# The rounding number of the FFN weights' FP4 quantisation, taken from a bit mask and a maximum on VectorE to a quadratic on ScalarE

## The chip, the cores and the metric

One core of one Trainium2 chip. The metric is the device time of one execution in microseconds (us), the median of several. The engines are called PE (TensorE, matmul), PEld (its weight loads), DVE (VectorE), ACT (ScalarE), POOL (GpSimd) and SP (SyncE, which issues the transfers here).

## The reference

One block of a network on x of shape (4, 1024, 256), with a context of shape (4, 154, 192):

```
x = x + attention(layernorm(x), ctx)      # 16 heads of 64, 154 keys
x = x + ffn(layernorm(x))                 # 256 -> 704 -> 256
ffn(x) = fp4_linear(silu(fp4_linear(x, w_gate)) * fp4_linear(x, w_up), w_down)

def fp4_quant_dequant(x):                 # on activations and on weights, blocks of 16
    scale = max(max|xb| / 6, 1e-12)
    xn = xb / scale
    q = GRID[searchsorted(MID, |xn|)] * sign(xn) * scale
    # GRID 0, .5, 1, 1.5, 2, 3, 4, 6
```

So every weight matrix of the FFN (704x256 twice, 256x704 once) is quantised once per launch: divided by its block's scale, rounded to a grid whose step is 0.5 below 2, 1 from 2 to 4 and 2 from 4 to 6, and multiplied by the scale again.

## The kernel before, in words

The 4096 rows are 32 tiles of 128, called t here. Each engine has its own instruction stream, written out in one order by hand, and semaphores tie the streams together. A tile's attention takes 8 slots, k = 0 to 7, one for each pair of heads; slot 0.4 is slot 4 of tile 0. In a slot PE makes the scores of a pair (line 1286), DVE takes their negated maximum (`largest_score`, L909), ACT makes the exponentials (L670), DVE inverts their sums (L892), POOL multiplies (`normalise`, L521). PE turns the probabilities around (L1298), ACT copies them from PSUM (`weights_hi`, tile `pT_hi`, L597), DVE writes what that copy lost (`weights_lo`, tile `pT_lo`, L783), and PE attends with both (L1313 to L1315). The same pair of high part on ACT and low part on DVE, L597 and L783, takes every product that PE must read again: `q_hi` and `q_lo`, `B_sb`, `WGU`, `WD`. The layer norm, the FFN's gate and up products and its down product of earlier tiles are put between the slots; each engine runs one stream, so what stands behind a waiting instruction waits too.

The quantisation of the FFN's weights lies beside the attention of tiles 0 and 1 and the first slot of tile 2, in 8 chunks, c0 to c7: six of 128x512 (gate and up side by side) and two of 128x704 (down). Slots are counted on from tile 0. `RAW_AT = [0, 1, 3, 5, 6, 8, 11, 14]` says in which slot a chunk's block scales are made on DVE (`chunk_scales`: L810, L816, L818). One slot later, so in slots 0.1, 0.2, 0.4, 0.6, 0.7, 1.1, 1.4 and 1.7, DVE divides (`chunk_divide`, L824) and makes the rounding number c(n) of each element n (`chunk_rounder`: `power`, L830, keeps the exponent bits; `rounder`, L835, multiplies by 1.5*2^22 and takes the maximum with 1.5*2^22). POOL then adds c, subtracts c and multiplies by the scale (`round_chunk`, helper `fp4`: L486, L490, L492); in tile 0 in the same slot, in tile 1 in the slot after. Adding and subtracting c rounds n to the step of c's binade. The chunk alternates between two tiles for c, `hc` and `hn`. Later PE turns the chunk around (L1163), and ACT and DVE split it into `WGU` or `WD` (`chunk_hi`, `chunk_lo`), in the slots of `TURN_AT = [3, 4, 5, 7, 9, 12, 14, 15, 18, 19]`.

The orders that matter to the change, for a slot in which a chunk is divided:

- ACT, tile 0: exponentials (L670), `weights_hi` of pair k-2 (L597), layer norm 1 out (L626, slots 2 and 4), `xT_hi` (slot 6), `q_hi`, the halves of V, K and B for this batch, `chunk_hi`.
- ACT, tile 1: `weights_hi` of pair k-3, `q_hi`, [layer norm 2 out in slot 5], exponentials, layer norm 1 out (slot 4), `chunk_hi`.
- DVE, tile 0: L909, L824, L892, L830, L835, `pT_lo`, layer norm statistics, `q_lo`, `chunk_scales` of the next chunk, the low parts of B, `chunk_lo`.
- DVE, tile 1: L892, `pT_lo`, L909, `q_lo`, `chunk_lo`, statistics, L824, L830, L835, `chunk_scales`.
- POOL, tile 1: L521 of pair k-1, then the chunk divided one slot earlier.

The FFN's activations go through the same `power` and `rounder` on DVE in every tile; that isn't touched.

Of the kernel before, what the change touches and what calls it, by code (L numbers as in the profile page):

```python
# [6 lines left out]
ACT = mybir.ActivationFunctionType  # L7
# [6 lines left out]
BLOCK = 16  # L14
# [9 lines left out]
def xattn_ffn_kernel(nc: bass.Bass, x, ctx_768, Wq, Wk, Wv, Wo, bo, w_gate, w_up, w_down, out):  # L24
# [31 lines left out]
    with ExitStack() as stack:  # L56
# [3 lines left out]
        def sem(name):  # L60
            return stack.enter_context(nc.semaphore(name))
# [30 lines left out]
        small = sb("small", [P, 24])  # L92
        ln = [[small[:, 10 * i + a:10 * i + b] for a, b in ((0, 6), (6, 8), (8, 9), (9, 10))] for i in range(2)]
        st1, mv1, rs1, nm1 = ln[0]
        st2, mv2, rs2, nm2 = ln[1]
        pow_arg, minus = small[:, 20:21], small[:, 21:22]

        x1_both = sb("x1_both", [P, 2, C])
        x1 = [x1_both[:, i, :] for i in range(2)]
# [55 lines left out]
        st_y = [sem("st_y0"), sem("st_y1")]  # L155
        pad_p, ident_p, pow_p, kpad_p = (sem(n) for n in ("pad_p", "ident_p", "pow_p", "kpad_p"))
        pre_mm, pre_ev, wq_hi, wq_lo, ppad_v = (sem(n) for n in ("pre_mm", "pre_ev", "wq_hi", "wq_lo", "ppad_v"))
        raw_v, raw_p, raw_mm, raw_hi, raw_lo = (sem(n) for n in ("raw_v", "raw_p", "raw_mm", "raw_hi", "raw_lo"))
        k_mm, k_hi, k_lo, v_mm, v_ev = (sem(n) for n in ("k_mm", "k_hi", "k_lo", "v_mm", "v_ev"))
        b_mm, b_hi, b_lo = sem("b_mm"), sem("b_hi"), sem("b_lo")  # L160
        ln1_v, ln1_p, xln1_a = sem("ln1_v"), sem("ln1_p"), sem("xln1_a")
# [309 lines left out]
        def _(pool):  # L471
# [1 line left out]
            pool.wait_ge(ident_p, 1)  # L473
            pool.affine_select(out=ident[:, :], in_=ident[:, :], compare_op=ALU.not_equal, fill=1.0,
                               base=0, pattern=[[-1, P]], channel_multiplier=1).then_inc(ident_p, 1)
            for v, value in ((pow_arg, -0.5), (minus, -1.0)):
                pool.memset(v, value).then_inc(pow_p, 1)
            pool.memset(hn[:, F:FP], 0.0).then_inc(pad_p, 1)

# [22 lines left out]
                pool.wait_ge(done, before + 3)  # L502
                pool.tensor_tensor(nm, nm, rs, ALU.mult).then_inc(done, 1)

            pool.wait_ge(pow_p, 2)
            for n in range(2):
                rstd(mv1, rs1, nm1, (ln1_v, 3 * n + 3), ln1_p, 4 * n)
                pool.memset(K_sb[n][:, :, :].bitcast(F32), 0.0).then_inc(kpad_p, 1)
# [85 lines left out]
        def _(act):  # L594
# [85 lines left out]
            def first(t, setup):  # L680
                for k in range(SLOTS):
                    exponentials(t, k)
                    if k >= 2:
                        weights_hi(t, k - 2)
                    if k == 2:
                        layer_norm1_out(2, 0)
                    if k == 4:
                        layer_norm1_out(t + 3, 1 - t)
                    if k == 6:
                        hi_part(xT_all(0), parts(xT_bank(setup), 4), (xT_mm, 2), xT_hi)  # L690
                    if q_unit(t, t, k) is not None:
                        q_hi_part(t, q_unit(t, t, k))
                    for job in jobs_at(setup, k):
                        take_hi(job, 0)
                    if t == 0 and k == 0:
                        act.wait_ge(pre_mm, CTX_T)
                        for r in range(2, CTX_T):
                            context(r)
                    if turn_at(t, k, 0) is not None:
                        chunk_hi(turn_at(t, k, 0))  # L700

            def step(pair, par, own=True, before=True, gate=True, down=True, out_=True, ahead=True, queries=True,
# [3 lines left out]
                for k in range(SLOTS):  # L706
# [72 lines left out]
        def _(dve):  # L779
# [142 lines left out]
            def first(t, setup):  # L922
                for k in range(SLOTS):
# [23 lines left out]
            def step(pair, par, own=True, before=True, gate=True, down=True, out_=True, ahead=True, queries=True,  # L947
# [3 lines left out]
                for k in range(SLOTS):  # L951
# [551 lines left out]
```

## Time and profile before

| | |
|---|---|
| runs | 870.67, 871.01, 872.89 us, median 871.01 |
| profiled execution | 872.43 us, of which the span from first to last instruction is 870.6 us |
| busy share of the span | PE 96%, DVE 82%, POOL 62%, ACT 60% |
| granted PE clock | 0.988 of full speed on average |
| PE busy in 40 equal slices | 7877899999999999999999999999999999999986 |
| DVE busy in 40 equal slices | 4889788878787888877878888887777888888886 |

The digits are tenths of a slice of 21.8 us. In the first four slices PE isn't full, from the sixth it is. The chain of work that ended last is followed back from the last instruction, at each step to what released it; "idle ... until" and "[0.40 <-ACT ...]" name what ended an engine's idle time. Neighbouring instructions of one engine overlap in the records by about 0.1 us.

### The profile page before, as it was taken

The numbers are of one execution on the slowest core, as the hardware profiler recorded it, in microseconds if no ns is written. First come the engines' busy times: TensorE is split into PE (matmuls) and PEld (weight loads), VectorE is DVE, ScalarE is ACT, GpSimd is POOL, SyncE is SP. The second block draws the span as 40 slices with busy tenths as digits, with TensorE's granted clock in tenths as the row PEclk, the third lists the DMA queues.
The fourth block names the chain that finished last, engine by engine and source line by source line (L and its number), as shares of the span: only waits on it lengthen the run. The fifth ranks groups of instructions, "written<-read, shape, count | busy, mean of one in ns | idle before, by whom it ended". The sixth has DMA issues, their size and how long they took to land.

```text
span 870.6 us, 19198 instructions
## 1 busy us (share of the span) xinstructions
PE 832.2 (96%) x6302; PEld 807.1 (93%) x6302; DVE 710.1 (82%) x2155; ACT 524.8 (60%) x1868; POOL 541.3 (62%) x810
## 2 busy tenths in 40 slices
PE   7877899999999999999999999999999999999986
PEld 7766899999999999999998999999998999999985
DVE  4889788878787888877878888887777888888886
ACT  5554566666676666666666666667656666665530
POOL 3768577765455766665653766665554666666644
PEclk8999999999999999999999999999999999999998
DMA  6320000002010000001111000000200000000000
GB/s 180 103 64 7 8 19 14 26 14 55 15 43 26 13 26 8 25 14 26 43 43 26 14 25 13 26 14 7 62 7 26 7 26 14 19 14 14 7 7 19
DMA packets 20756, 24.30 MB, mean 28 GB/s; under 512 B 2061, under 2 KB 18869, under 8 KB 20661
## 3 DMA queue, kind: packets, MB, share of 16 engines
q1 hardware_dynamic: 19573, 22.04, 8.9%
q8 instruction: 52, 0.85, 0.4%
q10 hardware_dynamic: 1088, 1.05, 0.4%
q14 instruction: 43, 0.35, 0.1%
HBM read 18.89 MB, written 4.19 MB: 27 GB/s over the span
## 4 chain that ended last, share of the span: by engine, by line
PE 81%; DVE 13%; issue 2%; ACT 2%; POOL 1%; DMA 1%; SPq 0%; DVEq 0%; ACTq 0%
PE ps_g L1333 12%; PE ps_s L1286 11%; PE ps_q L1241 10%; PE ps_t L1298 8%; PE ps_o L1313 7%; PE ps_o L1315 7%; PE ps_o L1314 7%; PE ps_g L1197 3%; PE ps_m L1163 3%; PE ps_m L1347 3%; PE ps_m L1349 3%; PE ps_m L1348 2%; PE ps_g L1186 2%; PE ps_q L1186 1%; DVE pT_lo L783 1%
## 5 line engine op out<-in xcount | busy, mean ns | idle before, releaser
L521 POOL TENSOR_TENSOR probs<-probs,rsum 128x308 f32<-128x308 f32 x256 | 180.6, 706 | 214.9 <-DVE rsum L892 214.4
L670 ACT ACTIVATE probs<-ps_s,negmax 128x154 f32<-128x154 f32 x512 | 195.0, 387 | 196.9 <-DVE negmax L909 195.7
L909 DVE TENSOR_REDUCE negmax<-ps_s 128x2 f32<-128x308 f32 x256 | 121.0, 473 | 76.3 <-PE ps_s L1286 75.2
L1313 PE MATMUL ps_o<-B_sb,pT_lo 128*128 128x256 f32 x640 | 180.8, 282 | 0.8 <-DVE x_both L1013 0.5
L1315 PE MATMUL ps_o<-B_sb,pT_hi 128*128 128x256 f32 x640 | 180.5, 282 | 0.0
L1314 PE MATMUL ps_o<-B_sb,pT_hi 128*128 128x256 f32 x640 | 180.3, 282 | 0.0
L783 DVE TENSOR_TENSOR pT_lo<-ps_t,pT_hi 128x256 fp32r<-128x256 f32 (+1 forms) x256 | 122.9, 480 | 30.4 <-ACT pT_hi L597 30.3
L1333 PE MATMUL ps_g<-WGU,xqT_hi 128*128 128x352 f32 x504 | 131.9, 343 | 0.3 <-DVE eh L1036 0.3
L1298 PE MATMUL ps_t<-ident,probs 128*128 128x128 f32 x640 | 113.0, 274 | 16.7 <-DVE pT_lo L783 14.5
L1313 PEld LDWEIGHTS ps_o<-B_sb,pT_lo 128*128 128x128 f32 x640 | 120.8, 189 | 1.3 <-issue 0.7
L1315 PEld LDWEIGHTS ps_o<-B_sb,pT_hi 128*128 128x128 f32 x640 | 121.3, 190 | 0.0
L1314 PEld LDWEIGHTS ps_o<-B_sb,pT_hi 128*128 128x128 f32 x640 | 121.2, 189 | 0.0
L597 ACT ACTIVATE pT_hi<-ps_t 128x256 fp32r<-128x256 f32 (+1 forms) x256 | 111.4, 435 | 6.6 <-PE ps_t L1298 3.4
L670 ACT ACTIVATION_READ_ACCUMULATOR probs<-ps_s,negmax 128x1 f32 x512 | 100.9, 197 | 0.0
L1298 PEld LDWEIGHTS ps_t<-ident,probs 128*128 128x128 f32 x640 | 74.6, 140 | 22.8 <-issue 17.6
L1286 PE MATMUL ps_s<-K_hi,q_lo 128*128 128x308 f32 x256 | 87.1, 340 | 0.0
L1333 PEld LDWEIGHTS ps_g<-WGU,xqT_hi 128*128 128x128 f32 x504 | 82.0, 189 | 0.6 <-DVE eh L1036 0.5
L1241 PE MATMUL ps_q<-xT_hi,Wq_lo 128*128 128x256 f32 x254 | 79.1, 312 | 3.5 <-DVE q_lo L783 2.0
L486 POOL TENSOR_TENSOR hn<-hn,hc 128x704 f32<-128x704 f32 x31 | 52.9, 1707 | 45.6 <-DVE hc L835 45.6
L1333 PE MATMUL ps_g<-WGU,xqT_lo 128*128 128x352 f32 x252 | 81.2, 322 | 0.0
L1286 PE MATMUL ps_s<-K_hi,q_hi 128*128 128x308 f32 x256 | 77.9, 304 | 0.0
L1286 PE MATMUL ps_s<-K_lo,q_hi 128*128 128x308 f32 x256 | 77.8, 304 | 0.0
(236 smaller groups left out, 2199.3 us busy)
## 6 DMA issues: line engine op xcount, KB each, us to landing
xa<-in_x_dram SPq DMA_DIRECT2D x33, 128.0 KB, 2.1
xr<-in_x_dram SPq DMA_DIRECT2D x32, 128.0 KB, 2.0
out_dram<-y_xn SPq DMA_DIRECT2D x30, 128.0 KB, 1.7
W_sb<-in_L_xattn_Wk_dram SPq DMA_DIRECT2D x3, 768.0 KB, 5.7
W_sb<-in_L_xattn_Wv_dram SPq DMA_DIRECT2D x2, 768.0 KB, 6.2
probs<-in_L_xattn_Wq_dram ACTq DMA_DIRECT2D x4, 256.0 KB, 4.9
Wo_sb<-in_L_xattn_Wo_dram SPq DMA_DIRECT2D x1, 1024.0 KB, 6.4
W_sb<-in_L_xattn_Wv_dram SPq DMA_DIRECT2D x2, 384.0 KB, 3.5
```

The lines of the kernel that those rows point to most:

```text
L521: pool.tensor_tensor(unit, unit, rsum[:, 2 * u:2 * u + 2].unsqueeze(2) .to_broadcast([P, 2, M]), ALU.mult).then_inc(norm_p, 1)
L597: act.activation(dst, src, ACT.Copy).then_inc(done, 1)
L670: ins = act.activation(probs[:, h, 0:M], ps_s[k % 2][:, s * M:(s + 1) * M], ACT.Exp, bias=negmax[:, h:h + 1], accum_out=sums[:, h:h + 1])
L783: dve.tensor_tensor(dst, src, hi.bitcast(F32), ALU.subtract).then_inc(done, 1)
L909: dve.tensor_reduce(negmax[:, 2 * k:2 * k + 2], ps_s[k % 2][:, 0:UM].rearrange("p (h m) -> p h m", h=2), AX_X, ALU.max, negate=True).then_ ...
L1241: ins = pe.matmul(q_bank(pair, u)[:, 0:2 * P], Wq_sb[w][:, k, u * P:(u + 1) * P], xT[x_][:, k, :], start=(i == 0), stop=(i == len(terms) - 1))
L1286: ins = pe.matmul(ps_s[u % 2][:, 0:UM], q_sb[a][:, u, par * P:(par + 1) * P], K_sb[b][:, u, :], start=(i == 0), stop=(i == len(terms) - 1))
L1298: ins = pe.transpose(ps_t[:, j * P:(j + 1) * P], probs_rows[:, at:at + P], ident[:, :])
L1313: pe.matmul(ps_o[:, 0:C], lo[:, j, :], w[:, 0:C], start=first, stop=False)
L1314: pe.matmul(ps_o[:, 0:C], hi[:, j, :], w[:, C:2 * C], start=False, stop=False)
L1315: ins = pe.matmul(ps_o[:, 0:C], hi[:, j, :], w[:, 0:C], start=False, stop=last)
L1333: ins = pe.matmul(ps[:, 0:2 * QF], x_[:, k, :], WGU[:, k, a, :, q * QF:(q + 1) * QF], start=(i == 0), stop=(i == len(terms) - 1))
```

## The change

Six copies of the pair L830/L835 of 128x512 and two of 128x704 leave DVE. In their place ACT squares n into the same tile (`Square`) and makes c = n^2 * 2^21/3 + 2^24/3 from it in place (`Identity` with an immediate scale and a per-partition bias, a new column `grid` that POOL sets at the start). For |n| below 2, from 2 to 4 and from 4 to 6 this c lies in the binades whose steps are 0.5, 1 and 2. A new semaphore raw_a counts ACT's two steps: the first waits for DVE's divide, the second for the first, and POOL's add waits for the second. On ACT the two stand behind `weights_hi` in tile 0, and behind the exponentials in tile 1, ahead of layer norm 1 out, `q_hi` and all that follows. In the diff the added `chunk_rounder` and its two calls are ACT's, the removed one and its two calls DVE's, in each case first in tile 0 (function `first`), then in `step`.

```diff
-            for v, value in ((pow_arg, -0.5), (minus, -1.0)):
+            for v, value in ((pow_arg, -0.5), (minus, -1.0), (grid, 2.0**24 / 3.0)):
                 pool.memset(v, value).then_inc(pow_p, 1)
...
-            pool.wait_ge(pow_p, 2)
+            pool.wait_ge(pow_p, 3)
...
             def round_chunk(c):
                 n = RAW_N[c]
                 fp4(raw[RAW_IN[c]][:, 0:n], raw_c[c % 2][:, 0:n], raw_s[c % 2][:, 0:n // BLOCK], raw_p, 3 * c,
-                    (raw_v, 6 * c + 6))
+                    (raw_a, 2 * c + 2))
...
+            def chunk_rounder(c):
+                n = RAW_N[c]
+                act.wait_ge(raw_v, 4 * c + 4)
+                act.activation(raw_c[c % 2][:, 0:n], raw[RAW_IN[c]][:, 0:n], ACT.Square).then_inc(raw_a, 1)
+                act.wait_ge(raw_a, 2 * c + 1)
+                act.wait_ge(pow_p, 3)
+                act.activation(raw_c[c % 2][:, 0:n], raw_c[c % 2][:, 0:n], ACT.Identity, bias=grid, scale=2.0**21 / 3.0)\
+                   .then_inc(raw_a, 1)
...
                     exponentials(t, k)
                     if k >= 2:
                         weights_hi(t, k - 2)
+                    if raw_at(t, k, 1) is not None:
+                        chunk_rounder(raw_at(t, k, 1))
...
                     if own:
                         exponentials(t, k)
+                    if raw_at(t, k, 1) is not None:
+                        chunk_rounder(raw_at(t, k, 1))
...
-            def chunk_rounder(c):
-                n = RAW_N[c]
-                v = raw[RAW_IN[c]][:, 0:n]
-                power(v, raw_c[c % 2][:, 0:n], (raw_v, 6 * c + 4), raw_v)
-                rounder(raw_c[c % 2][:, 0:n], raw_v, 6 * c)
...
                     invert_sums(t, k)
-                    if raw_at(t, k, 1) is not None:
-                        chunk_rounder(raw_at(t, k, 1))
...
                         chunk_divide(raw_at(t, k, 1))
-                        chunk_rounder(raw_at(t, k, 1))
```

## Rows read from the trace of the kernel before

**Rows 1.** Busy time by stretch: us, engine busy (instructions), granted clock, DMA share, GB/s.
```profile
25.00:96.00 71.00, 54.17 (x363) 47.63 (x363) 62.19 (x146) 38.37 (x129) 53.61 (x64) 0.95 0.13 40
96.00:870.60 774.60, 758.02 (x5824) 740.36 (x5824) 635.12 (x1977) 474.04 (x1709) 476.54 (x724) 1.00 0.08 21
```
**Rows 2.** Busy time of line L830 in all eight chunks (25:83 and 86:90).
```profile
sum 62.00, DVE 4.98; mean DVE 2.49
```
**Rows 3.** The same for line L835.
```profile
sum 62.00, DVE 5.67; mean DVE 2.83
```
**Rows 4.** ACT's groups by shape: busy us, mean ns | idle before.
```profile
L638 ACT ACTIVATE Wq_hi<-probs 128x512 fp32r<-128x512 f32 x4 | 2.5, 624 | 0.0
L744 ACT ACTIVATE y_xn<-x_both 128x256 f32<-128x256 f32 x29 | 12.0, 413 | 0.0
L626 ACT ACTIVATE xa<-xa,small 128x256 f32<-128x256 f32 x33 | 19.7, 598 | 2.3 <-POOL small L503 2.3
L626 ACT ACT_TABLE_LOAD x1 | 1.3, 1283 | 2.8 <-issue 2.8
```
**Rows 5.** Slots 0.1 and 0.2: start, duration us, in order of time [idle before].
```profile
26.74 0.41 DVE L783 TENSOR_TENSOR q_lo<-ps_q,q_hi 128x256 fp32r<-128x256 f32 x1
28.86 1.23 DVE L824 SCALAR_TENSOR_TENSOR y_xn<-y_xn,scales 128x512 f32<-128x512 f32 x1
32.95 0.39 DVE L783 TENSOR_TENSOR q_lo<-ps_q,q_hi 128x256 fp32r<-128x256 f32 x1
33.49 0.35 PE L1241 MATMUL ps_q<-xT_hi,Wq_lo 128*128 128x256 f32 x1 [0.34 <-DVE q_lo L783]
```
**Rows 6.** Slot 0.4, in order of time.
```profile
41.40 0.38 ACT L597 ACTIVATE pT_hi<-ps_t 128x256 fp32r<-128x256 f32 x1
41.66 0.60 ACT L626 ACTIVATE xa<-xa,small 128x256 f32<-128x256 f32 x1
43.93 0.69 DVE L783 TENSOR_TENSOR B_sb<-ps_g,B_sb 128x512 fp32r<-128x512 f32 x1 [0.40 <-ACT B_sb L597]
45.13 0.47 DVE L909 TENSOR_REDUCE negmax<-ps_s 128x2 f32<-128x308 f32 x1
```
**Rows 7.** Slot 0.6, POOL and DVE in order of time.
```profile
54.80 1.29 POOL L490 TENSOR_TENSOR eh<-eh,hn 128x512 f32<-128x512 f32 x1
54.92 1.21 DVE L816 TENSOR_SCALAR scales<-scales 128x32 f32<-128x32 f32 x1
```
**Rows 8.** Slot 0.7, the low part of B.
```profile
61.27 0.68 DVE L783 TENSOR_TENSOR B_sb<-ps_g,B_sb 128x512 fp32r<-128x512 f32 x1
```
**Rows 9.** Slot 1.1, divide and the next pT_lo.
```profile
65.18 0.81 DVE L824 SCALAR_TENSOR_TENSOR eh<-eh,scales 128x512 f32<-128x512 f32 x1
67.79 0.56 DVE L783 TENSOR_TENSOR pT_lo<-ps_t,pT_hi 128x384 fp32r<-128x384 f32 x1 [0.42 <-ACT pT_hi L597]
```
**Rows 10.** Slots 1.4 and 1.5.
```profile
74.43 0.86 DVE L824 SCALAR_TENSOR_TENSOR VT<-VT,scales 128x704 f32<-128x704 f32 x1
75.17 0.39 ACT L597 ACTIVATE pT_hi<-ps_t 128x256 fp32r<-128x256 f32 x1
76.42 0.40 DVE L783 TENSOR_TENSOR pT_lo<-ps_t,pT_hi 128x256 fp32r<-128x256 f32 x1
79.39 1.42 DVE L920 TENSOR_SCALAR scales<-scales 128x16 f32<-128x16 f32 x1
```
**Rows 11.** Slot 1.7 and after it.
```profile
86.27 1.05 DVE L824 SCALAR_TENSOR_TENSOR VT<-VT,scales 128x704 f32<-128x704 f32 x1
89.56 1.71 POOL L486 TENSOR_TENSOR VT<-VT,hn 128x704 f32<-128x704 f32 x1
95.91 0.44 PE L1298 MATMUL ps_t<-ident,probs 128*128 128x128 f32 x2 [1.49 <-POOL probs L521]
```
**Rows 12.** Two stretches with a lowered PE clock, columns as in rows 1.
```profile
34.40:40.10 5.70, 5.70 (x33) 5.34 (x33) 3.81 (x10) 3.55 (x10) 3.65 (x7) 0.75 0.10 28
81.20:85.00 3.80, 3.52 (x17) 3.55 (x18) 3.06 (x9) 1.89 (x7) 2.92 (x4) 0.56 0.00 0
```

More of the change, by code:

```diff
@@ L95, in xattn_ffn_kernel @@
         st2, mv2, rs2, nm2 = ln[1]
-        pow_arg, minus = small[:, 20:21], small[:, 21:22]
+        pow_arg, minus, grid = small[:, 20:21], small[:, 21:22], small[:, 22:23]
         x1_both = sb("x1_both", [P, 2, C])
@@ L157, in xattn_ffn_kernel @@
         pre_mm, pre_ev, wq_hi, wq_lo, ppad_v = (sem(n) for n in ("pre_mm", "pre_ev", "wq_hi", "wq_lo", "ppad_v"))
-        raw_v, raw_p, raw_mm, raw_hi, raw_lo = (sem(n) for n in ("raw_v", "raw_p", "raw_mm", "raw_hi", "raw_lo"))
+        raw_v, raw_a, raw_p, raw_mm, raw_hi, raw_lo = (sem(n) for n in ("raw_v", "raw_a", "raw_p", "raw_mm", "raw_hi", "raw_lo"))
         k_mm, k_hi, k_lo, v_mm, v_ev = (sem(n) for n in ("k_mm", "k_hi", "k_lo", "v_mm", "v_ev"))
@@ L853, in chunk_scales @@
                 largest(raw[RAW_IN[c]][:, 0:RAW_N[c]], hri[:, 0:nb], raw_v)
-                fp4_scales(hri[:, 0:nb], raw_s[c % 2][:, 0:nb], hri[:, 0:nb], raw_v, 6 * c)
+                fp4_scales(hri[:, 0:nb], raw_s[c % 2][:, 0:nb], hri[:, 0:nb], raw_v, 4 * c)
             def chunk_divide(c):
@@ L858, in chunk_divide @@
                 v = raw[RAW_IN[c]][:, 0:n]
-                scaled(v, v, hri[:, 0:n // BLOCK], raw_v, 6 * c)
-            def chunk_rounder(c):
-                n = RAW_N[c]
-                v = raw[RAW_IN[c]][:, 0:n]
-                power(v, raw_c[c % 2][:, 0:n], (raw_v, 6 * c + 4), raw_v)
-                rounder(raw_c[c % 2][:, 0:n], raw_v, 6 * c)
+                scaled(v, v, hri[:, 0:n // BLOCK], raw_v, 4 * c)
             def chunk_lo(n):
```

## The prediction

> **What bounds the kernel now.** I read the page's busy shares and its 40 slices first, then the busy times by stretch, then the chain of waits and the instructions in order of time from 14 to 112 us, since the change lives there. From 96 us to the end PE is busy for 758.0 of 774.6 us; before that it isn't: from 25 to 96 us it works 54.2 of 71 us, while DVE works 62.2, POOL 53.6 and ACT 38.4 [rows 1]. All eight chunks are in this stretch. In the chain of waits most pieces of it are DVE's, with ACT's exponentials and high parts between them. So it is a stretch in which the order on DVE and ACT sets the time, and whatever it gains or loses shifts everything behind it one for one: the steady part has no transfer or clock of its own to hide it in. A quick reading is "DVE has 9 us idle in 71, ACT 33, move work from one to the other". The rows of single slots say something else, and the sum goes by them.
>
> **What is removed.** The bit mask takes 4.98 us in the eight chunks [rows 2] and the maximum 5.67 [rows 3], together 10.65, some 1.3 us a chunk. Part of that is not work but waiting for POOL, which the changed kernel loses as well.
>
> **What is added on ACT.** The trace has no Square. Its nearest row is L638, an SBUF to SBUF copy of 128x512 with immediate operands: 0.624 us. L744 does 128x256 in 0.413 [rows 4]; the difference is 0.211 for 256 columns, so 704 columns take 0.62 + 0.16 = 0.78. The Identity has one per-partition operand. L626 has two and takes 0.598 against L744's 0.413 [rows 4], so one costs 0.09: 0.72 for 512 columns, 0.87 for 704. Two neighbours overlap by about 0.1 (`pT_hi` starts at 41.40 and lasts 0.38, the next starts at 41.66 [rows 6]), but the Identity waits for the Square's end, some 0.06 later. A pair thus takes 0.68 + 0.62 = 1.3 us of ACT's stream for 512 columns, and 0.84 + 0.77 = 1.6 for 704: 6 * 1.3 + 2 * 1.6 = 11.0 us. Bounds: no ACT row on whole partitions from SBUF is shorter than L744, twice 0.41, so 0.8; above, both at L626's price stretched to 512 columns, twice 0.81, so 1.6 (for 704: 1.0 and 1.9). I take 1.3 and 1.6, as L638 is the same shape.
>
> ScalarE: Activation LUTs of the Trainium skill, "Rules for kernel authors", puts multiply, add and maximum on VectorE, not on ScalarE. That rule speaks against this change. By it nothing is won even in busy time, and the trace agrees: 10.65 us leave DVE, waits for POOL included, and 11.0 come onto ACT.
>
> **Slot by slot**, in the times of the profiled execution; d is what a slot adds to everything after it.
>
> *Slots 0.1 and 0.2.* In 0.1 ACT is free for the pair at 25.2, when its exponentials are done, is through at 26.5, and only then makes `q_hi`, to 26.9. DVE's `q_lo`, at 26.74 before [rows 5], goes at 26.93: d = +0.2. In 0.2 the divide ends at 30.09 [rows 5], 0.2 later 30.3; the pair runs to 31.7, layer norm 1 out takes 0.5, `q_hi` ends at 32.5. DVE has meanwhile done `pT_lo` and the statistics and takes `q_lo` at 32.5 where it was 32.95. PE waited for exactly this, at 33.49 [rows 5], and slot 0.3 hangs on PE's products behind it. Net of both slots: -0.4.
>
> *Slot 0.4.* DVE already waits 0.40 for ACT's half of B [rows 6], which stands behind `pT_hi`, layer norm 1 out, `q_hi` and V. The divide is long done when the pair would start, at 41.66, so ACT's whole queue moves by 1.3, DVE's low parts behind it and the next L909, at 45.13 before [rows 6], too. What DVE saves becomes waiting. d = +1.3.
>
> *Slot 0.6.* `xT_hi` comes 1.3 later, to 54.1; DVE's `xT_lo` stood at 53.62, so 0.5 is late there. But the scales behind it were held anyhow: L816 on 128x32 takes 1.21 us and ends with POOL's L490 [rows 7], and POOL's add starts hardly later than before (c ready at 53.55). d = +0.2, between 0 and 0.5.
>
> *Slot 0.7.* ACT: `pT_hi` to 59.8, the pair to 61.1, then B's half to 61.7. DVE's low part, at 61.27 before [rows 8], goes at 61.75: d = +0.5.
>
> *Slot 1.1.* The divide ends at 65.99 [rows 9]; the pair to 67.35, `WGU`'s half, then `pT_hi` to 68.3. DVE waited for `pT_hi` already and ran `pT_lo` at 67.79 [rows 9]: d = +0.5.
>
> *Slot 1.4.* The dear one. The divide comes late on DVE and ends at 75.29 [rows 10]; ACT has its exponentials done before, and before the change went straight on with layer norm 1 out (0.5), `WGU`'s half (0.27) and `pT_hi` at 75.17 [rows 10]. Now these three stand behind an instruction that waits for the divide: the pair lasts from 75.35 to 76.95, and `pT_hi` starts at 77.7. `pT_lo`, 76.42 before [rows 10], goes at 78.15: +1.7. Behind it DVE's small L920 took 1.42 us [rows 10] while POOL had its 704-column steps, and POOL keeps its times; a little of the lateness is hidden under that. d = +1.3 (1.0 to 1.7).
>
> *Slot 1.7.* Divide ends at 87.32 [rows 11]. The pair ends at 89.1, so POOL's add starts at 89.15, not at 89.56 [rows 11]: its long chain to the probabilities that PE waits for at 95.91 [rows 11] is 0.4 shorter. DVE's `pT_lo` behind the delayed `pT_hi` is 1.2 later, but PE had 1.49 of waiting there, so PE would arrive at about 95.6. d = -0.3.
>
> The memset on POOL is one column at the start, long before POOL's first wait for data ends: nothing, and under 0.1 if that cover were gone. The new semaphore wait of POOL is the old one with another sender.
>
> Sum: -0.4 + 1.3 + 0.2 + 0.5 + 0.5 + 1.3 - 0.3 = **+3.1 us**. The profiled execution took 872.43, 1.4 over the median 871.01; the shift goes onto the median: **874.1**. With the pair at its lower bound (0.5 less in six of the terms) the sum is about 0, 871; with its upper bound about +5, 876.
>
> **Rivals.**
>
> *PE's clock (the other side).* Twice in this stretch PE fell from the upper level (2.4 GHz) toward the lower (1.2 GHz): a mean grant of 0.75 over 34.4 to 40.1 and of 0.56 over 81.2 to 85.0 [rows 12], each time behind a gap of PE. At the upper level the first would be 5.7 * 0.25 = 1.4 us shorter and the second 3.52 * 0.44 = 1.5. PE's idle gaps move: in slot 0.2 `pT_lo` comes over a microsecond earlier and splits the gap. If both falls go, 874.1 - 2.9 = 871.2, not slower. It decides if neither gap reaches the old length. Against it: the second gap stays, and by my times the first is merely shifted.
>
> *More falls of the clock.* PE's gaps before `pT_lo` of 1.4 and 1.7 become 1.7 and 1.2 us longer, and could each bring a fall. At the price of the two falls above, 1.4 or 1.5 each, some of it hidden behind DVE: +2, 876.
>
> *DVE's relief is kept.* If ACT's lateness mostly falls into DVE's other waits, part of the 10.65 reaches the end. In slots 0.2, 0.6 and 0.7 DVE has no wait for ACT, which is for it; about 1.2 each there and half the losses of 0.4, 1.1 and 1.4 give -4 + 1.6 = -2.5, and with less blocking by POOL -4: 867 to 868.5. Against it: three of the eight slots show DVE waiting for ACT already or come out so above.
>
> *Table loads.* If Square isn't held beside Exp, each chunk takes two loads of 1.28 us [rows 4], 16 * 1.28 = 20.5 on top: 894.6. ScalarE: Activation LUTs of the Trainium skill, "Table sets", names the cheap functions that are in every set without naming square, and says that the compiler puts a load before a function that is missing. One load serves Exp, Tanh, Copy and Identity in this kernel; no run here shows Square.
>
> **How the numbers follow.** ACT's queue as summed: 0.52, of it 0.37 above and 0.15 below the bound; the clock recovers: 0.14; more falls: 0.18; relief kept: 0.12; table loads: 0.04. What a measurement of this kernel can tell from no change is about 0.3%, 2.6 us. Slower (above 873.6): 0.37 + 0.18 + 0.04 = 0.59. Faster (below 868.4): 0.10 of the relief and 0.02 of the clock, 0.12. Same: the rest, 0.29. The range runs from 869 to 877.5: it leaves out the table loads, most of the kept relief and two falls at full price, and takes in both bounds of the pair.
>
> **What would show it.** No second ACT_TABLE_LOAD; Square near 0.62 and 0.78 us, Identity near 0.72 and 0.87. DVE's busy time 10 us less, ACT's 11 more. DVE's waits for ACT between 25 and 92 us grow by more than 10 us, above all for `pT_hi` and for B's half, and ACT waits for L824 in slot 1.4. The L909 of slot 0.5 starts some 0.9 later than at 45.13, the L1298 at 95.91 some 3 later, and from there all is shifted alike. I am wrong if the lateness at 96 us is under 1 or over 5 us; wrong in the mechanism if ACT's `pT_hi` of slot 1.4 isn't late.

## The result, and the profile after

The changed kernel takes 875.42 us (median of 6 runs, 874.11 to 876.10) against 870.90 for the kernel before on the same chip; the ratio is 1.0041, 95% interval [1.0028, 1.0055]. A second batch (e9 below) gives 1.0037 [1.0023, 1.0051]. So it is slower by 3.2 to 3.6 us by the ratios (by the medians 4.5 in the first batch, 3.5 in the second); +3.1 us and 874.1 were forecast.

The profiled execution took 876.1 us, its span is 874.3. Its busy time by stretch, columns as in [rows 1]:

```profile
25.00:99.00 74.00, 56.84 (x356) 49.39 (x355) 50.02 (x124) 48.01 (x142) 52.21 (x64) 0.88 0.13 39
99.00:874.30 775.30, 760.22 (x5835) 742.86 (x5833) 636.56 (x1985) 475.27 (x1714) 476.35 (x724) 0.99 0.08 21
```

Against [rows 1] DVE is 12 us less busy and ACT 10 us more (over the whole span 11.1 less and 10.5 more), in a stretch that has grown from 71 to 74 us; what lies behind it is nearly unchanged, 775.3 for 774.6 us. ACT's new groups by shape, with the one table load of the kernel:

```profile
L669 ACT ACTIVATE hn<-hn,small 128x512 f32<-128x512 f32 x3 | 2.2, 723 | 0.1
L666 ACT ACTIVATE hn<-eh 128x512 f32<-128x512 f32 x2 | 1.3, 633 | 0.1
L669 ACT ACTIVATE hc<-hc,small 128x704 f32<-128x704 f32 x1 | 0.9, 881 | 0.0
L666 ACT ACTIVATE hc<-VT 128x704 f32<-128x704 f32 x1 | 0.8, 791 | 0.8 <-DVE VT L839 0.8
L626 ACT ACT_TABLE_LOAD x1 | 1.3, 1283 | 2.8 <-issue 2.8
```

Slot 0.4, in order of time, answering to [rows 6]:

```profile
40.38 0.38 ACT L597 ACTIVATE pT_hi<-ps_t 128x256 fp32r<-128x256 f32 x1
40.64 0.64 ACT L666 ACTIVATE hc<-x_both 128x512 f32<-128x512 f32 x1
41.32 0.72 ACT L669 ACTIVATE hc<-hc,small 128x512 f32<-128x512 f32 x1
41.95 0.59 ACT L626 ACTIVATE xa<-xa,small 128x256 f32<-128x256 f32 x1
42.84 0.42 DVE L798 TENSOR_TENSOR q_lo<-ps_q,q_hi 128x256 fp32r<-128x256 f32 x1 [1.62 <-ACT q_hi L597]
44.21 0.69 DVE L798 TENSOR_TENSOR B_sb<-ps_g,B_sb 128x512 fp32r<-128x512 f32 x1 [0.95 <-ACT B_sb L597]
45.41 0.47 DVE L918 TENSOR_REDUCE negmax<-ps_s 128x2 f32<-128x308 f32 x1
```

Here the whole case can be read. The pair occupies ACT from 40.64 to 41.95, 1.31 us, and layer norm 1 out, which followed `pT_hi` at once in [rows 6], follows it. DVE has lost its 1.2 us of work and waits 1.62 + 0.95 us for ACT instead. All of DVE's waits for ACT of this stretch (the exponentials left out) were 1.5 + 0.7 + 0.4 = 2.6 us before; they are now 18.7:

```profile
DVE pT_lo L798 <- ACT pT_hi L597: 10.5, 8, 2.7
DVE q_lo L798 <- ACT q_hi L597: 3.0, 2, 1.6
DVE B_sb L798 <- ACT B_sb L597: 2.6, 3, 1.2
DVE small L819 <- ACT xa L626: 1.3, 1, 1.3
DVE xT_lo L798 <- ACT xT_hi L597: 1.3, 1, 1.3
```

Slots 1.1, 1.4 with 1.5, and 1.7 with what follows, answering to [rows 9 to 11]:

```profile
69.59 0.56 DVE L798 TENSOR_TENSOR pT_lo<-ps_t,pT_hi 128x384 fp32r<-128x384 f32 x1 [2.19 <-ACT pT_hi L597]
...
77.16 0.79 ACT L666 ACTIVATE hc<-VT 128x704 f32<-128x704 f32 x1 [0.81 <-DVE VT L839]
79.53 0.37 ACT L597 ACTIVATE pT_hi<-ps_t 128x256 fp32r<-128x256 f32 x1
79.93 0.42 DVE L798 TENSOR_TENSOR pT_lo<-ps_t,pT_hi 128x256 fp32r<-128x256 f32 x1 [2.72 <-ACT pT_hi L597]
82.75 1.14 DVE L929 TENSOR_SCALAR scales<-scales 128x16 f32<-128x16 f32 x1
...
92.37 1.68 POOL L486 TENSOR_TENSOR VT<-VT,hn 128x704 f32<-128x704 f32 x1 [0.96 <-ACT hn L669]
93.08 0.56 DVE L798 TENSOR_TENSOR pT_lo<-ps_t,pT_hi 128x384 fp32r<-128x384 f32 x1 [2.46 <-ACT pT_hi L597]
93.78 0.41 PE L1304 MATMUL ps_t<-ident,probs 128*128 128x128 f32 x2 [2.41 <-DVE pT_lo L798]
```

And three stretches in which PE's clock was lowered: slot 0.6, slot 1.6, and slots 2.0 and 2.1. Slot 1.6 had a lowered clock before the change too ([rows 12], its second stretch); slot 0.3, the first one there, has a full clock now.

```profile
50.90:59.10 8.20, 7.95 (x30) 6.00 (x31) 5.94 (x12) 4.64 (x11) 4.30 (x4) 0.58 0.10 32
84.30:88.30 4.00, 3.75 (x17) 3.78 (x18) 2.74 (x9) 1.89 (x7) 2.41 (x4) 0.50 0.00 0
93.50:99.20 5.70, 5.42 (x33) 5.45 (x34) 3.20 (x10) 3.02 (x12) 5.54 (x6) 0.70 0.02 4
```

**Slot lengths.** The start of the maximum of the scores (L909, in the others L918 and so on) marks each slot. The distance from one to the next, worked out from the instructions in order of time, in us. The slots of e7 and of e10 to e12 that matter are given with these runs. Slots 0.0, 0.5, 1.2, 1.3, 2.0 and 2.3 are the same in nearly all.

| slot | before | after | e9 (again) | e2 both | e1 neither | e3 behind | e4 | e5 | e6 | e8 |
|---|---|---|---|---|---|---|---|---|---|---|
| 0.1 | 4.58 | 4.47 | 5.01 | 5.41 | 3.72 | 3.21 | 4.48 | 4.18 | 4.81 | 4.43 |
| 0.2 | 5.93 | 5.45 | 5.57 | 5.92 | 4.92 | 5.19 | 5.44 | 8.44 | 5.56 | 5.95 |
| 0.3 | 5.69 | 4.90 | 4.90 | 6.51 | 5.33 | 5.55 | 4.90 | 4.91 | 4.91 | 4.92 |
| 0.4 | 4.98 | 6.28 | 6.28 | 6.27 | 4.97 | 5.53 | 6.28 | 6.27 | 6.27 | 4.99 |
| 0.6 | 7.53 | 8.20 | 7.68 | 7.99 | 6.70 | 5.69 | 8.09 | 8.17 | 7.71 | 7.54 |
| 0.7 | 4.30 | 4.73 | 4.73 | 4.73 | 3.63 | 6.63 | 4.74 | 4.30 | 4.73 | 4.30 |
| 1.0 | 2.00 | 2.01 | 2.82 | 2.54 | 3.14 | 4.04 | 2.00 | 2.98 | 2.82 | 1.99 |
| 1.1 | 3.79 | 4.21 | 4.87 | 4.50 | 3.79 | 3.79 | 4.22 | 4.34 | 4.88 | 3.80 |
| 1.4 | 3.57 | 5.27 | 5.27 | 5.33 | 2.76 | 3.74 | 3.58 | 3.58 | 5.28 | 3.58 |
| 1.5 | 4.51 | 4.06 | 4.06 | 4.22 | 4.98 | 5.19 | 4.52 | 4.52 | 4.08 | 4.56 |
| 1.6 | 3.84 | 3.98 | 2.84 | 2.85 | 3.26 | 3.99 | 3.27 | 3.26 | 2.85 | 3.27 |
| 1.7 | 4.10 | 5.25 | 5.06 | 5.13 | 3.35 | 3.34 | 4.36 | 4.35 | 5.08 | 4.36 |
| 2.1 and 2.2 | 8.32 | 8.20 | 6.87 | 7.53 | 8.59 | 8.67 | 8.35 | 8.35 | 6.89 | 8.34 |

### The profile page after: what moved, and what is told of

It reads as the page before. It is cut to its first block, busy times and chain, and to the rows that moved or that the text cites. A ratio compares the mean times of both kernels' runs of the same rounds, so it can differ in the third digit from the quotient of the medians.

```text
span 874.3 us, 19207 instructions
## 1 busy us (share of the span) xinstructions
PE 836.7 (96%) x6302; PEld 811.0 (93%) x6302; DVE 699.0 (80%) x2139; ACT 535.3 (61%) x1884; POOL 539.5 (62%) x811
## 4 chain that ended last, share of the span: by engine, by line
PE 82%; DVE 11%; ACT 3%; issue 2%; DMA 1%; POOL 0%; SPq 0%; DVEq 0%; ACTq 0%
PE ps_g L1339 12%; PE ps_s L1292 11%; PE ps_q L1247 10%; PE ps_t L1304 8%; PE ps_o L1319 7%; PE ps_o L1321 7%; PE ps_o L1320 7%; PE ps_g L1203 3%; PE ps_m L1169 3%; PE ps_m L1353 2%; PE ps_m L1355 2%; PE ps_m L1354 2%; PE ps_g L1192 2%; PE ps_q L1192 1%; DVE pT_lo L798 1%
## 5 line engine op out<-in xcount | busy, mean ns | idle before, releaser
L918 DVE TENSOR_REDUCE negmax<-ps_s 128x2 f32<-128x308 f32 x256 | 120.9, 472 | 76.5 <-PE ps_s L1292 75.4
```

Of the source, the lines that this page charges most:

```text
L918: dve.tensor_reduce(negmax[:, 2 * k:2 * k + 2], ps_s[k % 2][:, 0:UM].rearrange("p (h m) -> p h m", h=2), AX_X, ALU.max, negate=True).then_ ...
```

## The experiments

Theory Q says: what a slot gains or loses is decided by the queue on ACT in front of the high parts; DVE's work is hidden beside it. Theory C says: part of the difference is PE's clock. The experiments were built from the changed kernel with a letter for each chunk that says who makes c and where: A is ACT at the change's place, T is ACT at the slot's end, D is DVE, B both engines, N neither. In e1, e3, e7, e10 and e11 DVE also waits, before it makes the next chunk's scales, for its own divide of the chunk before.

**e1, neither engine makes c.**

```diff
+        WHERE = "NNNNNNNN"
...
+            for n in range(2):
+                pool.memset((hn, hc)[n][:, 0:F], 0.0)
...
-                    (raw_a, 2 * c + 2))
+                    (raw_v, RAW_V[c + 1]) if WHERE[c] in "DBN" else (raw_a, RAW_A[c + 1]))
```

With the letter N `RAW_V[c + 1]` is 4 * c + 4: POOL's add waits for DVE's divide alone.

> Leaves out the rounding number altogether: neither VectorE nor ScalarE makes c, POOL adds and subtracts a tile that is set to zero once at the start, so the FFN weights stay unrounded. It measures what the relief of DVE is worth when ACT gets nothing for it. Theory Q (position in ACT's queue): the relief is real but small, because in slots 0.4, 1.1, 1.4 and 1.7 DVE then waits for ACT's or PE's own tail: 864 to 867.5 us, 3.5 to 7 below before. Rival R (DVE's busy time on the path, 10.65 us): 860.5 or less. Rival P (DVE's pair costs nothing on the path): 870 to 871.

Measured: 865.86 us, ratio 0.9923 [0.9894, 0.9952], 5.4 us under before by the medians, 4.2 to 9.2 by the interval. DVE's relief is worth this at most, and not 10.65; at most, since POOL starts right behind the divide here and so has no c to wait for either. Slot 0.4 shows why: it doesn't get shorter at all, 4.97 for 4.98 us. DVE arrives earlier and waits longer for ACT's half of B (0.93 for 0.40 in [rows 6]):

```profile
40.12 0.42 DVE L811 TENSOR_TENSOR q_lo<-ps_q,q_hi 128x256 fp32r<-128x256 f32 x1 [0.34 <-ACT q_hi L605]
41.47 0.69 DVE L811 TENSOR_TENSOR B_sb<-ps_g,B_sb 128x512 fp32r<-128x512 f32 x1 [0.93 <-ACT B_sb L605]
```

Slot 1.1 doesn't get shorter either; 0.1, 0.2, 0.6, 0.7, 1.4 and 1.7 do, by 0.7 to 1.0 each. Slots 1.0 and 1.5, each behind such a slot, are 1.1 and 0.5 us longer and give part of it back.

**e2, both.** DVE's pair stays, ACT has one too.

```diff
+        WHERE = "BBBBBBBB"
...
+                if WHERE[c] == "B":
+                    dst = hqT[0][:, :, :].rearrange("p j n -> p (j n)")[:, 0:n]
+                    src = Wq_sb[0][:, 0, 0:n].bitcast(F32)
+                    act.wait_ge(wq_hi, KV)
+                act.wait_ge(raw_v, RAW_V[c] + 4)
+                act.activation(dst, src, ACT.Square).then_inc(raw_a, 1)
```

> The kernel before with DVE's mask and maximum in place, and beside them on ACT, at the changed kernel's places and behind the same divide, a Square and an Identity of the same sizes that read other data (query weights) and write a tile nobody reads yet. Theory Q: the slots are set by the later of two queues, ACT's with the pair in front of the high parts, DVE's as before; ACT's is the later in nearly all, so DVE's work is hidden beside it: 875 to 877 us, about the changed kernel. Rival S (the two costs add up: relief of DVE is worth some 4 to 5 us and ACT's pair costs 8 to 9): 879 to 880.

Measured: 874.37 us, ratio 1.0032 [1.0019, 1.0045], a little below what was expected and not to be told from the changed kernel's 1.0041. With DVE's 10 us of work put back the time isn't longer, and slots 0.4, 0.7 and 1.4 have 6.27, 4.73 and 5.33 us, the changed kernel's 6.28, 4.73 and 5.27. The sum of relief and cost, 879 to 880, is excluded. In these slots the two queues run side by side and the later one counts. In slots 0.1 to 0.3 DVE's work isn't hidden: they take 17.84 us together, the changed kernel's 14.82. Slot 0.2 is back at before's 5.92, since `pT_lo` stands behind the mask and the maximum again; PE is idle for 2.50 us before it, and its mean grant over slot 0.3 is 0.68. So that is where the changed kernel keeps a part of DVE's relief.

**e3, the pair behind.** In ACT's stream alone it moves.

```diff
+        WHERE = "TTTTTTTT"
...
                     if turn_at(t, k, 0) is not None:
                         chunk_hi(turn_at(t, k, 0))
+                    if raw_at(t, k, 1) is not None and WHERE[raw_at(t, k, 1)] == "T":
+                        chunk_rounder(raw_at(t, k, 1))
```

and in tile 1 to the next slot, ahead of layer norm 2 out and the exponentials.

> The changed kernel with ACT's pair moved back in ACT's stream only: in tile 0 to the end of the slot, behind q_hi, the halves of V, K, B and chunk_hi; in tile 1 to the next slot behind weights_hi and q_hi, ahead of the exponentials. Engines, operations and sizes are the changed kernel's. Theory Q: the loss was the position, so pT_lo, q_lo and B's low part no longer wait for the pair: 866 to 870.5 us, under the kernel before. Rival L (ACT's extra 11 us themselves cost): 873 to 876. A second danger: POOL gets c 1 to 2.5 us later and PE's turning of the chunk waits for it; if that decides, 871 to 873.

Measured: 878.32 us (873.27 to 878.92), ratio 1.0070 [1.0048, 1.0092]. The forecast failed, and the danger that it named (871 to 873) is seen in the trace, but the time lies far above its price too. ACT's queue is relieved (0.4 is 5.53, 1.4 is 3.74 us instead of 6.28 and 5.27; 0.1 even 3.21), but POOL gets c later and PE, whose stream is in order, stands before the turning of the chunk. PE, in order of time:

```profile
46.35 0.66 PE L1191 MATMUL ps_m<-ident,x_both 128*128 128x128 f32 x4 [3.20 <-POOL x_both L498]
58.21 1.12 PE L1191 MATMUL ps_m<-ident,eh 128*128 128x128 f32 x4 [3.10 <-POOL eh L498]
```

The profiled execution, 873.27 us, was the fastest of the five, with a mean grant of 0.990; the other four took 2.9 to 5.7 us more with 0.982 to 0.986, and no trace shows where. What follows: the position decides, yes, but it has two sides, and the change's own place served POOL. How much of the 7 us over before is POOL's lateness stays open.

**e4, the down weights' two chunks on DVE again.**

```diff
+        WHERE = "AAAAAADD"
```

> The changed kernel with the two 704-column chunks of the down weights, slots 1.4 and 1.7, back on DVE (mask and maximum); the six others stay on ACT. Theory Q: these two slots gave 1.25 and 1.15 us of the lateness in the trace, and the two lowered stretches of PE's clock behind them some more: 872 to 873.5 us. Rival L (cost in proportion to ACT's time, 3.3 of 11 us): 874.0 to 874.5.

Measured: 873.81 us, ratio 1.0029 [1.0015, 1.0043]. In the trace slots 1.4 and 1.5 are back at 3.58 and 4.52 us, exactly before's; the six other chunks keep the changed kernel's lengths. In time the two chunks give 0.7 to 1.6 us against the two batches of the changed kernel; the intervals overlap, so the trace shows the slots and the time doesn't settle the sum. It lies between the two ranges of the expectation.

**e5, slot 0.4 alone.**

```diff
+        WHERE = "DDADDDDD"
```

> The kernel before with one chunk alone done the new way, c2 in slot 0.4, where DVE already waited for ACT's half of B. Theory Q: the slot is 1.2 to 1.4 us longer and hardly anything else moves: 872.2 to 872.8 us. Rival L (an eighth of the whole change's lateness, since ACT's and DVE's times change by an eighth): 871.4 to 871.8. Told apart above all by the distance of the two L909 of slots 0.4 and 0.5 in the profile: 4.98 us before, 6.3 by theory Q.

Measured: 871.45 us, ratio 1.0012 [0.9996, 1.0029]. The median lies in rival L's range, the ratio puts it between the two, and the interval takes in both: the time tells nothing. By the slot it is Q: the two maxima stand 6.27 us apart.

```profile
40.97 0.47 DVE L935 TENSOR_REDUCE negmax<-ps_s 128x2 f32<-128x308 f32 x1
47.24 0.47 DVE L935 TENSOR_REDUCE negmax<-ps_s 128x2 f32<-128x308 f32 x1
```

The profiled execution was one of the three longest of its ten (875.4; seven lie between 870.1 and 872.9), with falls of the clock in slots 0.6 and 1.1 that before hadn't; slot 1.0 is 1.0 us longer at a full grant. Slot 0.2, 2.5 us longer though nothing was changed in it, waited for a load first: Wo was issued at 21.5 us and landed 8.9 us later, at 30.4, and PE's first product with it follows at once:

```profile
30.53 4.25 PE L1223 MATMUL ps_g<-Wo_sb,VT 128*128 128x256 f32 x10 [3.15 <-issue]
```

Before, the same load landed 6.4 us after its issue, at 27.4, and the product started at 28.08. Why it took longer here is not shown. One instruction stream thus spreads over more than this whole change.

**e6, PE's gaps filled in the changed kernel.**

```diff
+        FILL = {'x': (14, 8), (1, 5): (14, 11), (1, 6): (9, 11), (2, 0): (11, 12)}
...
+                pe.wait_ge(q_lo, done)
+                busy(ps_q, n)
```

> The changed kernel with matmuls that nobody reads put into four of PE's gaps (14, 14, 9 and 11 of 128x256 into a bank whose last product has been read), ahead of the turning of x in slot 0.6 and of the probabilities in slots 1.5, 1.6 and 2.0, where the trace shows 2.85, 2.70, 2.07 and 2.41 us of idleness and a lowered clock after three of them. Theory C (part of the lateness is PE's clock): the grant stays at 1.00 in 50.9 to 59.1, 84.3 to 88.3 and 93.5 to 99.2, slot 0.6 is about 0.5 us shorter and the stretch from slot 1.7 to 2.3 about 1 us: 872.5 to 874 us. Rival Q alone (queue only, the clock is beside the path): 875 to 876.

Measured: 874.82 us, ratio 1.0044 [1.0027, 1.0061]. Inconclusive in time, and against theory C as a price. The grant is 1.00 in all three stretches named, and slots 0.6 and 1.6 are 0.5 and 1.1 us shorter than in the first trace of the change; but slots 1.0 and 1.1, where nothing was filled, are 0.8 and 0.7 us longer. The trace of e9 has the same lengths in these four slots with no filling at all, though its grant is 0.78 in slot 0.6 and 0.77 in slot 1.6 where e6 has 1.00. Falls as mild as these cost the slots nothing; the first trace's 0.59 and 0.50 went with the longer ones.

**e7, two chunks only, at the slots' ends.**

```diff
+        WHERE = "TTDDDDDD"
```

> A version that should beat both: only c0 and c1 on ACT, at the end of the slot behind q_hi and the halves of V and B; the six others keep mask and maximum on DVE. In the kernel with all pairs at the slot's end these two slots were 1.4 and 0.7 us shorter, before POOL's lateness told in later ones. Theory Q: 868.5 to 870 us, 1.5 to 2.5 under before. Rival (the gain is lost again at PE, which waits for chunks 0 and 1 in slots 0.3 and 0.4, or by a fall of the clock): 871.

Measured: 870.50 us, ratio 0.9999 [0.9986, 1.0012]: by its time the rival, though neither of the causes that it named came first. Slot 0.1 has 3.20 us for 4.58, slot 0.2 7.14 for 5.93. PE:

```profile
26.22 0.36 PE L1269 MATMUL ps_q<-xT_hi,Wq_lo 128*128 128x256 f32 x1 [0.55 <-DVE q_lo L809]
29.68 3.37 PE L1225 MATMUL ps_g<-Wo_sb,VT 128*128 128x256 f32 x10 [2.51 <-issue]
```

No engine explains the 2.51 us before the first product with Wo; the load of Wo does. It was issued at 21.0 us and took 8.5 us to land, where before it took 6.4:

```profile
L384 SPq DMA_DIRECT2D Wo_sb<-in_L_xattn_Wo_dram x1: 1417/1417/1417, 21.0 to 21.0; - x1
DMA to landing us min/median/max: 8.5/8.5/8.5
```

Landing at 29.5, product at 29.68. The late landing belongs to this execution and to e5's, whose kernels differ in these slots; whether e7's other eleven executions had it is not shown.

**e8, before with its own two gaps filled.**

```diff
+        FILL = {(0, 3): (11, 0), (1, 6): (14, 11)}
```

> The kernel before with matmuls that nobody reads in two of PE's gaps: 11 of 128x256 ahead of the turning of pair 1's probabilities in slot 0.3, 14 ahead of the one of pair 4 in slot 1.6, that is in the gaps behind which its trace shows a grant of 0.75 and 0.56. Theory C (PE's falls lie on the path): slot 0.3 goes from 5.7 to some 4.9 us and slot 1.6 is 0.3 to 0.8 shorter: 869.5 to 870.5 us. Rival (the falls are beside the path, or only move): 871 to 871.6.

Measured: 870.39 us, ratio 0.9993 [0.9982, 1.0005]. The grants are 1.00 where [rows 12] has 0.75 and 0.56:

```profile
32.80:37.70 4.90, 4.83 (x37) 4.53 (x36) 3.70 (x10) 3.30 (x10) 3.63 (x7) 1.00 0.18 54
78.90:82.20 3.30, 2.93 (x23) 2.76 (x23) 3.02 (x10) 1.90 (x7) 2.42 (x4) 1.00 0.00 0
```

Slot 0.3 is 0.77 us shorter, 1.6 0.57, and 1.7 gives 0.26 back: 1.1 us between the two traces. So the falls of before's trace are worth 0.8 and 0.3 us and not the 1.4 and 1.5 of the prediction, which took all of PE's work for path. In time it can't be told from nothing. Nor is it shown that the filling brought it: e4, e5 and e7, with before's code in slot 1.6 and no filling, have 3.27, 3.26 and 3.31 us there, at grants of 1.00, 0.69 and 0.66.

**e9, the change again.** The changed kernel's instructions; no diff.

> The changed kernel once more, instruction for instruction, beside the others on one chip, for a second trace and a closer ratio. Theory Q: the lateness of slot 0.4 (+1.3), 0.7 (+0.4), 1.1 (+0.4), 1.4 and 1.5 together (+1.2) comes again to 0.1 us, since it is queue; that of slots 0.3, 0.6 and 1.7 to 2.2, which I put down to the clock, may differ by a microsecond: 874 to 875.5 us, ratio 1.003 to 1.005. Rival (all of it is fixed): every slot as in the first trace.

Measured: 874.47 us, ratio 1.0037 [1.0023, 1.0051]. Slots 0.4, 0.7, 1.4 and 1.5 are as in the first trace to 0.01 us. Slots 0.1, 0.6, 1.0, 1.1, 1.6 and 2.1 with 2.2 differ by +0.5, -0.5, +0.8, +0.7, -1.1 and -1.3. So slot 1.1, which the expectation counted among the queue's terms, did not come again: it is 1.1 us over before, not 0.4. The lowered grants lie differently too: milder in slots 0.6 and 1.6, new in 1.1 and 1.7, none in 2.1.

```profile
50.00:60.00 10.00, 8.56 (x44) 6.63 (x44) 8.12 (x16) 5.14 (x14) 4.31 (x4) 0.83 0.09 26
65.00:70.00 5.00, 3.34 (x15) 3.21 (x16) 2.95 (x8) 2.90 (x9) 3.63 (x7) 0.66 0.02 6
85.00:90.00 5.00, 4.21 (x25) 4.24 (x26) 4.89 (x15) 2.74 (x11) 3.16 (x6) 0.71 0.00 0
```

In the first trace the lateness at slot 2.3 is 4.24 - 0.35 (its later start) = 3.9 us, in this one 2.8. The queue's part (slots 0.4, 0.7, 1.4 and 1.5) is the same in both. The rest isn't all clock: slots 0.1 and 1.0 differ at a grant of 1.00 in both traces. In slot 1.0 DVE's small step on the next chunk's scales took 0.18 us in the first trace, where it came just before POOL's next instruction, and 1.07 in this one, where it came just behind it. First trace, then this one:

```profile
64.95 0.18 DVE L831 TENSOR_SCALAR gu<-scales 128x32 f32<-128x32 f32 x1
64.96 1.09 POOL L492 TENSOR_TENSOR y_xn<-y_xn,scales 128x512 f32<-128x512 f32 x1
...
64.69 1.06 POOL L498 TENSOR_TENSOR y_xn<-y_xn,scales 128x512 f32<-128x512 f32 x1
64.72 1.07 DVE L842 TENSOR_SCALAR gu<-scales 128x32 f32<-128x32 f32 x1
66.66 0.87 PE L1324 MATMUL ps_t<-ident,probs 128*128 128x128 f32 x3 [2.72 <-DVE pT_lo L809]
```

`pT_lo` stands behind that step, PE waits 2.72 us for it instead of 1.22, and the fall of the clock in slot 1.1 comes behind this gap. In slot 0.1 it is the divide: 0.69 us in the first trace, 1.18 in this one, and ACT's pair waits for it.

**e10, e7 with Wo loaded early.**

```diff
             load_xa(1, bass.ts(3, P))
+            sp.dma_start(Wo_sb[:, :, :], Wo.rearrange("(q p) n -> p q n", p=P)).then_inc(ld_wo, 16)
             sp.wait_ge(k_mm, 2)
...
-            sp.dma_start(Wo_sb[:, :, :], Wo.rearrange("(q p) n -> p q n", p=P)).then_inc(ld_wo, 16)
```

> The kernel with c0 and c1 alone on ACT at the slots' ends, and the load of Wo (1 MB) issued ahead of Wv's, at about 12 us instead of 21. In its trace the first product with Wo started at 29.7 us, later than before the change, behind 2.5 us of idleness of PE that no engine explains. Theory D (the gain of the two slots was lost to that transfer): slot 0.2 to 0.3 no longer stretches, and it takes 867 to 869 us. Rival E (the gap is ACT's V behind the exponentials, or the earlier load only delays Wv): 870 to 872.

Measured: 870.17 us, ratio 0.9985 [0.9975, 0.9996]: rival E's time, not theory D's. Slot 0.2 takes 4.68 us for e7's 7.14, so the transfer was what PE had stood before; but slot 0.4 takes 5.90 for 5.43. There ACT's layer norm waits for POOL, which got both chunks late; in e7 the same wait is 0.33 us, and what is added is POOL's own small step L505, 0.71 us for 0.19:

```profile
41.30 0.60 ACT L632 ACTIVATE xa<-xa,small 128x256 f32<-128x256 f32 x1 [0.79 <-POOL small L509]
```

**e11 and e12, the version that this points to, and the same with all chunks on DVE.**

```diff
+        WHERE = "TADDDDDD"
+        FILL = {(0, 3): (11, 0), (1, 6): (14, 11)}
```

In e12 the letters are `"DDDDDDDD"`; both have the early load of Wo.

> The version the runs point to: c0 on ACT at the end of slot 0.1, c1 on ACT at the changed kernel's place (so that POOL gets it no later), six chunks on DVE, Wo loaded early, and PE's two gaps of slots 0.3 and 1.6 filled. Theory Q with C: slots 0.1 and 0.2 give 1 to 1.5 us, the two falls of the clock 1.3: 868 to 869.5 us, ratio 0.997 to 0.9985. Rival (slot gains are lost again at ACT's layer norm in slot 0.4, which waits for POOL, as with both chunks at the slots' ends): 870 to 871.

> The same early load of Wo and the same two filled gaps with all eight chunks on DVE, so that what ACT's two chunks bring is told apart from the rest. Theory: the fills are worth 1.3 us in the trace and the early load little here, 869.5 to 870.3 us, 0.7 to 1.5 above the version with two chunks on ACT. Rival (the two chunks on ACT bring nothing): equal within 0.3 us.

Measured: 869.98 us, ratio 0.9987 [0.9974, 1.0000], and 870.02, ratio 0.9987 [0.9976, 0.9997]. Both forecasts of a gain from ACT's two chunks failed. The two kernels are equal: the two chunks on ACT bring nothing that a measurement can tell. In e11's trace slot 0.1 has 3.20 us for e12's 4.43, and 0.2 and 0.3 have 6.47 and 5.41 for 5.95 and 4.91, which leaves 0.2 us. What slot 0.1 gave is lost in slot 0.2, and not in slot 0.4 as the rival had it (4.97 us): ACT's pair of c0 ends at 27.28 us, ahead of the exponentials, and DVE waits 1.35 us for them. Both are 1.1 us (by the ratio) to 1.4 us (by the medians) under before, within the 0.3% that counts as no change. No version with c on ACT was found that is faster than the same kernel with c on DVE (e7 against before, e11 against e12).

## Why the prediction was right

By its own steps, against both traces of the change (first, second), in us:

| step | forecast | measured |
|---|---|---|
| pair on ACT, 512 / 704 columns | 1.3 / 1.6 | 1.31 / 1.6 |
| slots 0.1 and 0.2, with 0.3 behind them | -0.4 | -1.4, -0.7 |
| slot 0.4 | +1.3 | +1.3, +1.3 |
| slot 0.6 | +0.2 | +0.7, +0.15 |
| slot 0.7 | +0.5 | +0.4, +0.4 |
| slots 1.0 and 1.1 | +0.5 | +0.4, +1.9 |
| slots 1.4 and 1.5 | +1.3 | +1.25, +1.25 |
| slot 1.6 | 0 | +0.1, -1.0 |
| slot 1.7 to 2.2 | -0.3 | +1.0, -0.5 |
| sum | +3.1 | +3.9, +2.8 |

That the sum comes within a microsecond is in part luck: in the first trace two rows miss by 1.0 and 1.3 us, with opposite signs, and in the second trace slots 1.0 and 1.1 miss by 1.4. The queue's terms are what was forecast and came.

*The bound.* Right: the stretch from 25 to 96 us and the orders of DVE and ACT in it. The quick reading, idle ACT takes work from busy DVE, was rightly left: e1 shows that the 10.65 us taken off are worth 5.4 (4.2 to 9.2) even when ACT gets nothing, and e2 that DVE's 10 us, put back beside ACT's pair, make the time no longer.

*The prices.* The four shapes came out at 633 and 791 ns for Square and 723 and 881 for Identity, within 0.02 us of the forecast. ScalarE: Activation LUTs of the Trainium skill, "What ACT_TABLE_LOAD costs", gives 186 ns and 0.833 ns a column, and 93 ns for a pointer operand; the estimate from this is 612, 772, 705 and 865 ns. The runs lie 16 to 21 ns above that; the rule on the pointer operand is met (723 - 633 = 90).

*The queue terms.* Slots 0.4, 0.7 and 1.4 with 1.5 came as worked out, in the first trace and the second; in e2 1.4 with 1.5 is +1.5. Slot 1.1 came in the first trace alone (+0.4); in the second it and slot 1.0 have +1.9, for the reason given with e9. In 1.4 ACT waited 0.81 us for the divide, ran the pair and brought `pT_hi` so late that DVE waited 2.72; L929, behind it, took 1.14 instead of 1.42 us while POOL's steps ran, and 0.45 of 1.70 came back in 1.5. SBUF — State Buffer of the Trainium skill, "SBUF: two separate sides", says that VectorE and GpSimd share a port pair, and that for some forms of VectorE's instructions whichever of the two starts first holds it for its whole instruction while the other stands. The rows with e9 agree: one small DVE instruction of one stream took 0.18 us ahead of POOL's start and 1.07 behind it, and ended with POOL's.

*The clock terms.* Here sizes were off. The sum let both of before's falls stand; but the one of slot 0.3 is gone in both traces (4.90 for 5.69 us), which is 0.8 of the -1.4 and all of the -0.7. The rival on the clock had named the reason, that `pT_lo` comes earlier in slot 0.2 and splits PE's gap; the prediction set it aside as "merely shifted", and that step was wrong. PE is now idle once, for 1.67 and 1.88 us in the two traces, ahead of `q_lo`, where it was idle for 1.89 and 0.34 us ahead of `pT_lo` and `q_lo`; with DVE's pair back in e2 it is idle for 2.50 us and the fall is back. In return others come: in 0.6 and 2.1 in the first trace, in 0.6, 1.1 and 1.7 in the second. Both rivals on the clock were partly true at once and nearly cancelled. The step of slot 1.7 failed in the first trace: POOL's add began 4.06 us after the slot's maximum (92.37 - 88.31; before it was 89.56 - 85.09 = 4.47), which is the gain that was forecast, but PE, idle for 2.41 us before `pT_lo`, ran at a grant of 0.70 behind it and lost what POOL had gained. In the second trace slot 2.1 has its 2.59 us of before, slot 1.7 is 0.96 longer and slot 2.2 1.45 shorter, since PE no longer waits for POOL there: -0.5, the mechanism of the forecast. That the falls themselves cause these slots' differences was not shown by time: in e6 and e8 they are gone from the stretches named, and the ratios move by less than their intervals. The second trace's slots 0.1 and 1.0, +0.5 and +0.8 over the first, are neither queue as summed nor clock but DVE's instructions beside POOL's, which the sum counts in slots 0.6 and 1.4 and not there.

*The rivals.* Relief kept: e1 puts it at 5.4 us without ACT's cost, so it is real where ACT is free. In the changed kernel it is kept in slots 0.2 and 0.3 alone (-0.5 and -0.8 us against before). Table loads: none came. ScalarE: Activation LUTs of the Trainium skill, "Table sets", leaves open whether Square stands beside Exp; here it does, one load of 1.28 us in all.

*The signs.* DVE's waits for ACT grew by 16 us where over 10 were asked for; ACT waited for the divide in slot 1.4; the L1298 of 95.91 us stands at 100.19 in the first trace and 98.72 in the second (+4.3 and +2.8; some 3 were forecast). One sign failed: the maximum of slot 0.5 was to start 0.9 us later than 45.13 and starts at 45.41 and 45.70, since slots 0.1 to 0.3 gained more than 0.4.

*Not foreseen.* That ACT's place ahead of `q_hi` had a purpose: POOL and through it PE and the next layer norm want c early. My theory of position, carried to e3, gave 866 to 870.5 and got 878.3.

What stays open: how much of the time's difference is the clock, and how much the meeting of DVE and POOL. The spread of one kernel's runs (874.1 to 876.1; e5 870.1 to 877.1) is as large as the terms in question, and a profile shows one execution. Why the load of Wo landed 2 us later in e5's and e7's executions is not known.

## What to carry to other kernels

Ask of a moved operation not how idle its new engine is but what stands behind it in that engine's stream, who waits for that, and whether the operation itself must wait for something late (slot 1.4: 1.6 us of work behind a late divide cost 1.25). Busy time taken from the busier engine counts only in slots where its partner isn't already the later one; here about half of it. And before moving it further back, look at who needs its result early.

## What the runs showed of the hardware

One instruction stream, profiled twice, had PE's clock lowered in different places and by different amounts. The mean grant over slot 0.6 was 0.59 in one (length 8.20 us) and 0.78 in the other (7.68), over slot 1.6 0.50 (3.98) and 0.77 (2.84), over slot 2.1 0.62 (4.11) and 1.00 (2.59), over slot 1.1 1.00 (4.21) and 0.65 (4.87). A lowered grant did not always cost: slot 1.6 took 2.84 us at 0.77 and, in e6, 2.85 at 1.00.

A small DVE instruction can take six times as long beside one of POOL's: the same step on 128x32 numbers took 0.18 us and 1.07 us in the two profiles of one stream, with 0.04 us of difference in when the two engines met. Slot 0.3 shows the price. It is 4.90 us where that step takes 0.18 us and PE has its full clock, and 5.33, 5.41 and 5.55 us in e1, e11 and e10, where the step takes 0.60, 0.68 and 0.82.

The load of Wo, 1 MB, landed 6.0 to 8.9 us after its issue in the kernels that issue it at 19 to 22 us.

Most slots with a full clock and no such meeting repeat to 0.01 or 0.02 us between kernels (slot 0.4: 6.27 or 6.28 us in six of them). So with slot lengths a single profile tells more than the time of ten runs, as long as three kinds of slots are set apart: those with a lowered grant, those with a long small DVE instruction beside POOL, and those that wait for a load.
